# Layer 1's attention, two batches in flight against a pipeline over five batches

## What is computed

```python
x = x + pos_emb[:S]
w = x.reshape(B, S // 64, 64, 16, 8)                 # 8 windows of 64 tokens, 16 heads of 8
attn = softmax(einsum("bnqhd,bnkhd->bnhqk", w, w) * scale)
local = einsum("bnhqk,bnkhd->bnqhd", attn, w)        # local attention in a window
comp = conv(x, conv_w, stride 4)[:, :64] + conv_b    # 64 compressed keys
gt = concat([comp, global_memory])                   # 128 global keys, also the values
ga = softmax(einsum("bshd,bghd->bhsg", x, gt) * scale)
glob = einsum("bhsg,bghd->bshd", ga, gt)
mix = sigmoid(concat([local, glob]) @ gate_w + gate_b)
out = (mix * local + (1 - mix) * glob) @ out_w + out_b
```

## Time and profile before

| | |
|---|---|
| runs | 1667.65, 1663.0, 1660.94 us; median 1663.0 |
| profiled execution | 1656.41 us, span 1654.6 us |
| granted clock, mean of the span | 0.825 |
| PE busy | 78% |
| DVE, ACT, POOL busy | 53%, 29%, 36% |

### The profile page before, as it was taken

One profiled execution on the slowest core, in us unless ns is written; L12 is line 12 of the kernel. 1 busy time (PEld: TensorE's weight loads), 2 busy tenths in 40 slices (PEclk: granted clock), 3 DMA queues, 4 the chain that ended last, 5 costly groups with the idle time before them and its releaser, 6 DMA issues. The chain is left out here.

```text
span 1654.6 us, 22122 instructions
## 1 busy us (share of the span) xinstructions
PE 1287.4 (78%) x7540; PEld 761.0 (46%) x7540; DVE 876.8 (53%) x2160; ACT 482.9 (29%) x1073; POOL 599.5 (36%) x628
## 2 busy tenths in 40 slices
PE   2777777777774599849989899988988259999991
PEld 1334444444443356525464654646545135555551
DVE  3467787788764222233554555454443325566565
ACT  0122222222221155513324132231313014443441
POOL 1335565556453245522233234332330302212221
PEclk8899898998875699958878687686767579999996
DMA  6001101101111442211011010110000061111105
GB/s 246 20 0 37 50 20 50 37 27 46 31 44 34 142 137 69 66 52 41 9 53 47 14 47 20 52 49 14 27 14 25 21 172 33 38 34 39 33 22 163
DMA packets 93990, 85.83 MB, mean 52 GB/s; under 512 B 10265, under 2 KB 85402, under 8 KB 92970
## 3 DMA queue, kind: packets, MB, share of 16 engines
q1 hardware_dynamic: 84922, 65.93, 13.2%
q0 software_dynamic: 8704, 17.97, 3.4%
q10 hardware_dynamic: 256, 0.53, 0.1%
HBM read 55.93 MB, written 30.07 MB: 52 GB/s over the span
## 5 line engine op out<-in xcount | busy, mean ns | idle before, releaser
L1045 POOL DMA_INDIRECT slots<-pay,slot x128 | 133.8, 1046 | 226.0 <-issue 162.0
L1551 PE MATMUL bank<-consts,region 128*128 128x128 f32 x512 | 81.2, 307 | 110.3 <-POOL region L1082 110.3
L1060 POOL DMA_INDIRECT y<-region,xin x80 | 76.9, 961 | 196.2 <-ACT region L1290 175.6
L1661 PE MATMUL bank<-wgl,rows 128*128 x288 | 138.8, 605 | 5.8 <-ACT rows L1273 5.8
L1551 PEld LDWEIGHTS bank<-consts,region 128*128 128x128 f32 x512 | 71.8, 213 | 154.9 <-POOL region L1082 126.3
L1082 POOL TENSOR_TENSOR region<-region 128x512 f32<-128x512 f32 x64 | 83.9, 1312 | 138.2 <-DVE region L762 120.2
L1273 ACT ACTIVATE rows<-bank 128x256 f32<-128x256 f32 x216 | 81.3, 385 | 103.7 <-PE bank L1655 101.4
L1060 POOL DMA_INDIRECT y<-hh,region x64 | 61.5, 961 | 122.8 <-ACT hh L1290 108.2
L1406 ACT ACTIVATE w0uv<-bank 128x512 f32<-128x512 f32 x128 | 66.1, 602 | 119.2 <-PE bank L1828 119.2
L622 DVE TENSOR_TENSOR rows<-bank,w0uv 128x512 f32<-128x512 f32 x72 | 49.7, 691 | 95.8 <-PE bank L1661 72.3
L1864 PE MATMUL bank<-values_l,w0uv 64*128 64x17 f32 x1024 | 91.4, 328 | 3.1 <-issue 2.7
(11 more groups left out here) (305 smaller groups left out, 2658.1 us busy)
## 6 DMA issues: line engine op xcount, KB each, us to landing
xin<-slots SPq DMA_DIRECT2D x80, 65.0 KB
region<-slots SPq DMA_DIRECT2D x64, 65.0 KB
mrow<-mods SPq DMA_DIRECT2D x16, 256.0 KB, 4.2
xres<-x SPq DMA_DIRECT2D x16, 256.0 KB, 2.3
wgl<-in_wgl SPq DMA_DIRECT2D x1, 4096.0 KB
rows<-y SPq DMA_DIRECT2D x8, 512.0 KB, 4.2
wgl<-y SPq DMA_DIRECT2D x8, 512.0 KB, 7.5
wgl<-in_x SPq DMA_DIRECT2D x8, 256.0 KB, 3.0
```

The source lines that it names most:

```text
L1045: p.indirect_dma_start(io["slots"], bass.IndirectOffsetOnAxis(ap=slot[:, k, t:t + 1], axis=0), pay[:, k, t, :], None).then_inc(S["scattere ...
L1060: p.indirect_dma_start(io["y"], bass.IndirectOffsetOnAxis(ap=xins[par][:, h, k, P + 1:P + 2].bitcast(U32), axis=0), bYs[par][:, h, k, :], ...
L1551: ins = M(bank[7][:, tile(t)], pr[:, j % 2, tile(t)], center, start=(j == 0 and t == 0), stop=(j == DH - 1 and t == NT - 1), skip_group_ch ...
L1661: ins = M(bank[k][:, :], bT[:, k, tile(c)], wgl[:, bass.ds(ex_of[h][k], 1), c, :].squeeze(1), start=c == 0, stop=c == FC - 1)
```

## The change

Step i now runs for i from -2 to 9 and holds work of five batches: f = i+2 (front), a = i+1 (compress, keys, global scores by queries and their maxima), i (local scores by queries, exponentials, values), b = i-1 (turn_out, gate, project, residual, normalise), c = i-2 (modulate, logits, rank, place, scatter). A step is six rounds on banks 0 to 3: again and bias, exponentials, scores by queries in the same four banks, their maxima. Rounds 0 and 1 take the local scores of batch i, rounds 2 to 5 the global ones of batch a; again_global waits for the maxima of the round before (`bank_free`). The ring is gone; banks 4 to 7 serve all else.

attend_local works on units (l, t), half of a half batch: the values of both windows lie side by side, with zeros elsewhere, in a block of 128 rows and 34 columns, so that one matmul of 128 rows takes the place of two of 64. values_l moves to region and is cleared before the stage; local_values copies it in four parts instead of two, and norm_local works on a unit.

Lines that the diff takes from the steps are left out below, since the printed functions hold them.

```diff
--- before.py
+++ after.py
-        values_l = sb("values_l", [P, NT, H // 2, 2 * DH + 1])
+        values_l = region[:, 12:15, :].rearrange("p a n -> p (a n)")[:, 0:NT * H * (2 * DH + 1)].rearrange("p (t h c) -> p t h c", t=NT, h=H // 2)
...
+        UNIT_BANK = ((6, 7), (4, 6))
+        S_STEPS, E_STEPS, PV_STEPS, REC_STEPS, NEG_STEPS, VA_STEPS = 32, 32, 8, 5, 5, 5
...
+        def attention_rows(step):
+            for i in range(-2, NB + 2):
+                step(i)
+        def ok(b):
+            return 0 <= b < NB
...
+            def step(i):
+                a, b, c = i + 2, i - 1, i - 2
+                if ok(a):
+                    if a:
+                        sp.wait_ge(S["c_xh1"], a * NT)
+                        settled(sp)
+                    load_front(a)
+                if ok(c):
+                    sp.wait_ge(S["c_h2"], c * 2 + 2)
                     settled(sp)
+                    sp.dma_start(xres_of(c), X).then_inc(S["st_x1"], 16)
+                    sp.wait_ge(S["st_x1"], c * 16 + 16)
                     settled(sp)
+                if ok(b):
+                    sp.dma_start(X, xres_of(b)).then_inc(S["load_k"], 16)
+                    sp.dma_start(mrow[:, :, :].rearrange("p k d -> p (k d)"), io["mods"][1, b, :].partition_broadcast(P)).then_inc(S["load_k"], 16)
+                if ok(a):
+                    store_front(a)
+            attention_rows(step)
...
+            def max_global(b, t):
+                v.wait_ge(S["c_S"], scores_before(b, t + 1))
+                for g in range(NHG):
+                    V.tensor_reduce(maxg[:, t, g * QD:g * QD + HG], bank[g].rearrange("p (h k) -> p h k", h=HG),
+                                    axis=AX, op=ALU.max).then_inc(S["c_mx"], 1)
...
+            def norm_local(b, l, t):
+                v.wait_ge(S["c_al"], b * 4 + 2 * l + t + 1)
+                pv = bank[UNIT_BANK[l][t]][:, 0:H * (2 * DH + 1)].rearrange("p (h w c) -> p w h c", w=2, c=2 * DH + 1)
+                if b:
+                    v.wait_ge(S["c_ntr"], (b - 1) * 2 + l + 1)
+                rec = recl[:, t, :].rearrange("p (w h) -> p w h", w=2)
+                V.reciprocal(rec, pv[:, :, :, 2 * DH]).then_inc(S["c_rec"], 1)
+                v.wait_ge(S["c_rec"], b * REC_STEPS + 2 * l + t + 2)
                 for a in range(2):
                     half = slice(a * WIN, (a + 1) * WIN)
-                    V.tensor_tensor(nrm[half, l, :, :, :, :].rearrange("p w t h c -> p w (t h) c"), pv[half, :, :, a * DH:(a + 1) * DH],
-                                    bc(recl[half, :, :], DH, 3), ALU.mult).then_inc(S["c_nl"], 1)
+                    V.tensor_tensor(nrm[half, l, :, t, :, :], pv[half, :, :, a * DH:(a + 1) * DH],
+                                    bc(rec[half, :, :], DH, 3), ALU.mult).then_inc(S["c_nl"], 1)
...
+            def step(i):
+                a, b, c, f = i + 1, i - 1, i - 2, i + 2
+                if ok(b):
+                    norm_local(b, 1, 1)
+                if ok(c):
+                    modulate(c)
+                if ok(i):
                     max_local(i, 0)
+                if ok(a):
+                    global_keys(a, a % 2)
+                if ok(f):
+                    add_front(f)
+                if ok(i):
                     max_local(i, 1)
+                if ok(c):
+                    router(1, c, 0.0, 0)
+                if ok(a):
+                    max_global(a, 0)
+                if ok(f):
+                    stats_front(f)
+                if ok(c):
+                    router(1, c, 0.0, 1)
+                    place(1, c)
+                if ok(a):
+                    max_global(a, 1)
+                if ok(b):
+                    mix(b, b % 2)
+                if ok(i):
+                    norm_global(i, i % 2)
+                if ok(a):
+                    max_global(a, 2)
+                if ok(b):
+                    residual(b)
+                if ok(i):
+                    norm_local(i, 0, 0)
+                if ok(a):
+                    max_global(a, 3)
+                if ok(i):
+                    norm_local(i, 0, 1)
+                    norm_local(i, 1, 0)
+                if ok(f):
+                    positions(f, f % 2)
...
+            def step(i):
+                a, b, c, f = i + 1, i - 1, i - 2, i + 2
+                if ok(a):
+                    local_keys(a, a % 2)
+                if ok(b):
                     gated_out(b)
+                    difference(b, b % 2)
+                if ok(f):
+                    norm_front(f)
+                if ok(c):
+                    scatter(1, c, 0)
+                    scatter(1, c, 1)
+                if ok(b):
                     ln_scale("ln2_st", "ln2_rs", b + NB)
                     normalise("c_xh2", b)
+                if ok(c):
+                    scattered(1, c)
...
             def local_values(b):
+                a.wait_ge(S["c_va_t"], 2 * b + 2)
+                for w in range(2):
+                    keys = slice(w * WIN, (w + 1) * WIN)
+                    for k in range(2):
+                        o = w * (2 * DH + 1) + k * DH
+                        A.activation(values_l[keys, :, :, o:o + DH],
+                                     bank[4][keys, :].rearrange("p (t k h c) -> p k t h c", t=NT, k=2, c=DH)[:, k, :, :, :], ACT.Copy).then_inc(S["c_va"], 1)
...
+            def step(i):
+                a, b, c, f = i + 1, i - 1, i - 2, i + 2
+                if ok(i):
+                    less_max_global(i)
+                    exps(i, 0)
+                if ok(a):
+                    compressed(a)
+                if ok(b):
+                    mixed_T(b, b % 2, 0)
+                if ok(c):
+                    h2_T(c)
+                if ok(i):
+                    exps(i, 1)
+                if ok(b):
+                    mixed_T(b, b % 2, 1)
+                if ok(i):
+                    exps(i, 2)
+                    less_max_local(i)
+                if ok(b):
+                    gate_tanh(b)
+                if ok(c):
+                    second_exp(c)
+                if ok(i):
+                    exps(i, 3)
                     local_values(i)
+                if ok(c):
+                    second_copy(1, c)
+                if ok(i):
+                    exps(i, HG)
+                if ok(a):
+                    global_values(a)
+                if ok(i):
+                    exps(i, HG + 1)
+                if ok(f):
+                    modulate_front(f, f % 2)
...
+            def score_global(b, p, t):
+                if t == 0:
                     t_.wait_ge(S["c_gm"], b + 1)
+                for g in range(NHG):
+                    if b:
+                        t_.wait_ge(S["c_exp"], (b - 1) * UNITS + (2 + t) * NHG + g + 1)
+                    elif t:
+                        t_.wait_ge(S["c_mx"], (t - 1) * NHG + g + 1)
+                    M(bank[g], xTs[p][heads(g), tile(t)], gmk[p][heads(g), :, :], start=True, stop=True).then_inc(S["c_S"], 1)
+            def score_local(b, p, l):
+                if l == 0:
                     t_.wait_ge(S["c_xm"], b * HG + HG)
                 for t in range(2):
                     for w in range(2):
                         toks = slice((2 * l + t) * P + w * WIN, (2 * l + t) * P + (w + 1) * WIN)
+                        for g in range(NHG):
+                            if t == w == 0:
+                                t_.wait_ge(S["c_exp"], b * UNITS + l * NHG + g + 1)
+                            ins = M(bank[g][w * WIN:(w + 1) * WIN, t * 2 * P:(t + 1) * 2 * P], xTs[p][heads(g), toks],
+                                    xmk[p][heads(g), :, toks], start=True, stop=True)
+                            if t:
+                                ins.then_inc(S["c_S"], 1)
...
+            def bank_free(b, k, g):
+                if k < 3:
+                    t_.wait_ge(S["c_mx"], b * UNITS + (HG - 1 + k) * NHG + g + 1)
+                elif b + 1 < NB:
+                    t_.wait_ge(S["c_mx"], (b + 1) * UNITS + (k - 3) * NHG + g + 1)
+                else:
+                    t_.wait_ge(S["c_exp"], b * UNITS + (k - 1) * NHG + g + 1)
             def again_global(b, p, r):
                 for g in range(NHG):
-                    if r == 0:
-                        t_.wait_ge(S["c_mx"], b * UNITS + 11 + g)
-                    else:
-                        t_.wait_ge(S["c_exp"], b * UNITS + (r - 1) * NHG + g + 1)
+                    bank_free(b, r, g)
                     M(bank[g], gmk[p][heads(g), r, :], xTs[p][heads(g), :], start=True, stop=False)
+            def less_global(b, r):
...
+            def attend_local(b, l, t):
                 t_.wait_ge(S["c_exp"], b * UNITS + (HG + l) * NHG + NHG)
-                for t in range(2):
-                    for h in range(H // 2):
-                        o = (t * (H // 2) + h) * (2 * DH + 1)
-                        for w in range(2):
```

(81 more changed lines are left out.)

381 lines of the change are left out of this document (106 added, 275 removed).

## The result

The changed kernel took **1639.9 us** (median of four executions, 1631.4 to 1643.8) beside 1662.0 for the kernel before: a ratio of 0.986 (95% interval 0.981 to 0.990), 22 us less. The forecast was 1575, 88 less. The profiled execution took 1639.4 us, span 1637.5, at a mean granted clock of 0.842.

What follows compares the result with a forecast made beforehand. TensorE, at a mean clock of 0.76, was taken as the bound. Front 16.3, step ahead 21, step 0 53, six steps 342, step 7 43 and drain 64.5 gave 539.8 against 628.3, hence 1575 us, range 1535 to 1655.

Steps and rivals of the forecast that it cites:

- the other queues, at nothing: Work of VectorE, GpSimd, ScalarE and SP beside TensorE's chain: said to fit; GpSimd 24 us per step plus at most 6 waiting.
- the term of the clock: TensorE's clock in a step: 15% of the time low, turning 53.2 us into 57 us a step.
- the ends: Stage outside the six middle steps: front 16.3, step ahead 21, step 0 53, step 7 43, drain 64.5 us.
- The chain: Six rounds on banks 0 to 3, 7.86 us each, 47.2, plus 6.0 of overs: 53.2 us a step at full clock.
- the overs: TensorE work exceeding its windows under exponentials (2.1 us) and maxima (2.5 us), plus the turn between steps: together 6.0 us.
- 46.4 of work: TensorE's own pieces per step after the change, priced at 2.4 GHz and summed: 46.4 us.
- The rival of 0.94 us a unit: attend_local: 128-row weight loads cost 59 ns like 64-row ones, some 1.5 us a step less: 1565 us; chance 0.06.
- The clock as low as now, 67 us a step, 1650: Rival: TensorE's clock stays low half the time, end steps 15 us more: 1650 us; chance 0.18.
- Slower: Rival: clock falls in project, local units keep it down; 70% low gives 77 us a step, 1710 us; chance 0.10.
- A wait elsewhere that closes the chain: Rival: a wait through SP, gated_out and GpSimd's scatters closes a loop over six rounds: 1655 to 1665 us; chance 0.04.
- the signs of being wrong: Gates over 66 us apart, clock 0.75 or below, or TensorE waits beyond banks 0 to 3 over 3 us a step.

Runs made afterwards that it cites:

- after_2: The changed kernel itself, unedited, run again on a fourth chip: 1553.6 us, ratio 0.943 to the kernel before.
- no_scatter: Changed kernel without layer 1's 64 scatters, the slot table being filled at the start instead: 1558.8 us, ratio 0.945 to the kernel before.
- hold_no_scatter: no_scatter with TensorE held some 5 us ahead of project in six steps by six GpSimd operations: 1662.3 us, ratio 1.008 to the kernel before.
- hold_round3: no_scatter with TensorE held some 5 us ahead of again_global of round 3 by seven GpSimd operations: 1602.0 us, ratio 0.969 to the kernel before.
- late_scatter: Changed kernel, but layer 1's GpSimd waits for project before issuing batch c's eight scatters: 1632.8 us, ratio 0.989 to the kernel before.
- project_late: Changed kernel with project moved behind again_local of unit 1 instead of unit 0: 1682.3 us, ratio 1.014 to the kernel before.
- one_inc: Changed kernel with one increment of c_E per local unit of again_local instead of eight: 1558.8 us, ratio 0.944 to the kernel before.
- second_pay: Changed kernel with second buffers for h2, payload and slots, scatters a step later beside global-score rounds 2 and 3: 1549.0 us (0.941); with gaps 1597.7 (0.961).

## Why the prediction was wrong

The stage in the forecast's terms, with the gate taken 21 us into its step:

```
                                      forecast  result   after_2 (clean)
first load to compress                  16.3     16.4      16.4
compress to the first gate              95      102.7     102.9
six steps, gate to gate                342      386.7     313.6
last of these gates to expert stage     86.5    102.1      92.6
stage                                  539.8    607.9     525.5
```

**The step that failed is "the other queues, at nothing"**, and with it the term of the clock. The eight scatters were costed by GpSimd's time alone, as work that nobody waits for. In the result's condition they stop TensorE in five of the six steps, at the one place where it issues some 30 small products in 1.2 us; the increments that ScalarE waits for come when the last scatter has landed. I then took 15% of the time at the low clock; it was 27.3 us of 68, 40%, in four of the steps, and 32% over the six. The arithmetic of one step: 51.8 at the full clock, 27.3 / 2 = 13.7 for what the low clock adds, and a remainder of 2.6, which I put down to the gaps, 68.1. The six steps came to 64.5 us each for 57.

**The clock.** That a gap brings most of the fall is shown by no_scatter (0 us low in four steps, 3 and 10 in two) against hold_no_scatter (a gap put back by hand, 17 to 41). The narrow work alone brings some of it: of the 54 steps in the nine profiles without such gaps 35 have no low clock, 18 have 3 to 10 us of it and one has 20.5. The forecast's reading of the trace before, that x512 groups keep the clock up "even across a wait of 1.82 us", held in part where such a group follows: hold_round3 has 3 to 7 us low in four steps of six, 14 and 24 in the others. It said nothing about a gap ahead of project and the local units, and there 2.0 us are enough for 10 to 27.

**In the clean condition the forecast would have stood.** 1575 against a before of 1663 is 0.947; after_2 has 0.943 (0.938 to 0.948). That is partly luck: the six steps were put 28 us too long, the ends 14 too short. The chain held: 53.2 us forecast, 51.8 measured. Of the 1.4 us between them 0.9 is a slip in the overs: by the windows that the forecast states, 2.1 and 2.5 us, they come to 5.1 and not 6.0. TensorE reads 51.7 busy in these 51.8 us where I summed 46.4 of work. Busy here holds waiting: the eight records of a score group, 0.97 us where nothing holds them, read 2.59 busy in the result while three of their weight loads wait 0.2 us each for the exponentials. So the page can't confirm the 46.4.

```profile
1025.31 2.59 PE L1819 MATMUL bank<-rows,wsh 32*128 32x512 f32 x8
```

**attend_local.** A unit of 16 records was to take 16 x 0.123 = 2.0 us. Timeline of after_2, and of late_scatter at the low clock:

```profile
895.38 1.97 PE L1922 MATMUL bank<-region,w0uv 128*128 128x34 f32 x16
```

```profile
959.22 3.63 PE L1924 MATMUL bank<-region,w0uv 128*128 128x34 f32 x16
```

Merging two 64-row products into one of 128 rows gains nothing in this kernel. The forecast set the Trainium skill's rule against this ("TensorE: Matmul & The Clock Gate", Part 2, Step-by-step: the time to load weights doesn't depend on the number of rows), and that was a misreading. The rule is about the length of one load, and the trace of before agrees with it, 188 ns for 64 rows and 192 for 128:

```profile
L1864 PEld LDWEIGHTS bank<-values_l,w0uv 64*128 64x128 f32 x64 | 3.7, 188 | 0.6 <-issue 0.6
L1766 PEld LDWEIGHTS bank<-hT,convw 128*128 128x128 f32 x8 | 1.0, 192 | 0.4 <-issue 0.4
```

What differs is the distance between starts, 59 ns against 123, since the loads overlap. The rival of 0.94 us a unit took that distance for the length of a load.

**Drain and head.** From the start of the last local products to the expert stage 64.5 were forecast; 1251.8 to 1317.9 is 66.1. The other 14 us of the table's fourth row lie ahead of that, in the last step behind its gate: 22 forecast, 36.1 in the result, 26.8 in after_2. Before the first gate the pipeline fills 8 us slower than forecast, in both conditions; why was not looked into.

**The rivals.** "The clock as low as now, 67 us a step, 1650" came nearest in its numbers (64.5 a step, 1640), by a cause that it didn't name. "Slower", where the clock falls in project and the units keep it down, is what project_late shows in part: 60.8 for 51.8 in a step without scatters. A wait elsewhere that closes the chain was not seen. Of the signs of being wrong, gates over 66 us apart came true in four steps of six; the clock between the gates was 0.84 and not 0.75; and the time on TensorE that is no wait for banks 0 to 3 was there as "issue", 2.2 us between products and 3.8 between weight loads in the step shown, where the forecast had set 3. That is how the gaps were found.

**Left open.** What the condition is, the recording among its possible causes; how the kernel after does in it without scatters; why TensorE's increments wait for the scatters' landings in it; whether fewer increments help there (one_inc met only the clean one); how late_scatter or project_late do in the clean one.

## What to carry to other kernels

A gap on the bounding engine costs more than itself where narrow products follow (some 8 us a step beyond the gap, while one ahead of x512 products cost 2), so price it by the work behind it and put waits that can't be avoided ahead of wide work. In the condition with gaps indirect scatters did better beside few, large instructions (0.961 for 0.986). And when two unrelated edits both cure a fault, run the uncured kernel again on the same chip before believing either.

## What was not expected of the hardware

- One chip runs the same program in two conditions, at different times: on chip 11 second_pay took 1597.7 and 1549.5 us and the kernel before 1659.3 and 1647.6. Over all chips it is 1640 and 1554 us for the changed kernel, 1655 to 1662 and 1648 to 1650 for the one before. Whether the chip or the recording makes the difference is open. The sign is in the records: 707 to 770 of 1024 increments of layer 0's scatters, or all of them.
- With gaps, semaphore increments of TensorE appeared 0.3 to 0.5 us after the last recorded landing of eight scatters, some 6 us after the last weight load of their products, in five steps of five; VectorE's own chain (reciprocal L921, product L923) ran on meanwhile.
- The kernel before, whose clock was low anyway, lost nothing by its scatters in the clean condition (1.000, 0.999 to 1.002), nor did the kernel after (0.943 with, 0.945 without). In the condition with gaps the kernel before took 5 to 14 us longer and the changed one 86: the looser schedule's profile gave little sign of a cost that the tighter one feels.
